# A hand-written order of work in the attention slots of a transformer layer: row maxima joined at part 53, projections in parts 44 to 47, reciprocals at 45 and 46 and at part 0 of the next slot

## The reference, cut to what matters

```python
q = split_heads(x @ Wq.T + bq)
k = split_heads(x @ Wk.T + bk)
v = split_heads(x @ Wv.T + bv)
q_lr = jnp.einsum('bhtd,hdr->bhtr', q, Wq_lsr)
k_lr = jnp.einsum('bhtd,hdr->bhtr', k, Wk_lsr)
scores = jnp.einsum('bhir,bhjr->bhij', q_lr, k_lr) * scale
scores = jnp.where(causal_mask, jnp.float32(-jnp.inf), scores)
attn = jax.nn.softmax(scores, axis=-1)
y = jnp.einsum('bhij,bhjd->bhid', attn, v)
```

## Time and profile before

| | |
|---|---|
| median of 3 runs | 4275.05 us (4274.4 to 4277.15) |
| the profiled execution's own time | 4274.05 us |
| its span, first to last instruction | 4272.3 us |
| mean granted TensorE clock | 0.924 of full speed |
| busy: PE, DVE, ACT, POOL | 3743.8, 2262.9, 1473.4, 687.8 us |

### The profile page before, as it was taken

One profiled execution on the slowest core, in us unless ns is written; L12 is line 12 of the kernel. 1 busy time (PEld: TensorE's weight loads), 2 busy tenths in 40 slices (PEclk: granted clock), 3 DMA queues, 4 the chain that ended last, 5 costly groups with the idle time before them and its releaser, 6 DMA issues. The chain is left out here.

```text
span 4272.3 us, 57451 instructions
## 1 busy us (share of the span) xinstructions
PE 3743.8 (88%) x21481; PEld 2587.1 (61%) x21481; DVE 2262.9 (53%) x3990; ACT 1473.4 (34%) x2753; POOL 687.8 (16%) x859
## 2 busy tenths in 40 slices
PE   5898998998998989989989832799999999999990
PEld 3555555555555555555555422788888888888880
DVE  2565564664664655655646457444454444544445
ACT  1343442443443433434424400333333333333324
POOL 2021121121121211211211210011111111111100
PEclk8999999999999999999999965699999999999995
DMA  4224233133322332242331110333344333443328
GB/s 154 68 81 113 58 102 98 46 97 98 93 70 78 100 102 64 79 117 59 102 97 41 43 57 5 104 117 106 121 127 136 114 108 121 126 136 113 111 69 324
DMA packets 187321, 422.56 MB, mean 99 GB/s; under 512 B 39777, under 2 KB 42849, under 8 KB 178401
## 3 DMA queue, kind: packets, MB, share of 16 engines
q1 hardware_dynamic: 167408, 367.98, 28.7%
q0 software_dynamic: 14336, 34.09, 4.2%
q10 hardware_dynamic: 5376, 17.83, 1.0%
HBM read 245.70 MB, written 72.38 MB: 74 GB/s over the span
## 5 line engine op out<-in xcount | busy, mean ns | idle before, releaser
L841 DVE TENSOR_REDUCE max_slots<-shared_banks 128x1 f32<-128x512 f32 (+3 forms) x1536 | 786.0, 548 | 497.0 <-PE shared_banks L636 370.7
L792 ACT ACTIVATE probs<-scores_t 128x512 f32<-128x512 f32 (+3 forms) x1536 | 671.4, 492 | 661.5 <-PE scores_t L678 653.1
L1510 PE MATMUL m_ps_h<-m_tokens_t,m_w_parts 128*128 128x512 f32 x3072 | 740.0, 391 | 1.6 <-DVE m_tokens_t L1448 1.6
L1510 PE MATMUL m_ps_y<-m_w_parts,m_hidden_parts 128*128 128x512 f32 x3072 | 737.0, 390 | 0.5
L678 PE MATMUL scores_t<-q_operands,k_operands 128*128 128x512 f32 (+3 forms) x1536 | 570.5, 412 | 114.3 <-DMA q_operands<-minus_max 108.3
L1510 PEld LDWEIGHTS m_ps_y<-m_w_parts,m_hidden_parts 128*128 128x128 f32 x3072 | 575.5, 188 | 125.3 <-issue 6.3
L1510 PEld LDWEIGHTS m_ps_h<-m_tokens_t,m_w_parts 128*128 128x128 f32 x3072 | 575.6, 188 | 120.1 <-issue 2.0
L633 PE MATMUL shared_banks<-k_operands,q_operands 96*128 96x512 f32 (+3 forms) x1536 | 555.0, 392 | 13.8 <-DVE natural L834 7.9
L1417 ACT ACTIVATE m_hidden<-m_ps_h,m_b 128x512 f32<-128x512 f32 x256 | 176.6, 690 | 817.8 <-PE m_ps_h L1510 804.6
L678 PEld LDWEIGHTS scores_t<-q_operands,k_operands 128*128 128x128 f32 x1536 | 294.0, 207 | 237.0 <-DMA q_operands<-minus_max 114.9
L633 PEld LDWEIGHTS shared_banks<-k_operands,q_operands 96*128 96x128 f32 x1536 | 314.5, 206 | 193.2 <-issue 138.2
(11 more groups left out here) (202 smaller groups left out, 3139.4 us busy)
## 6 DMA issues: line engine op xcount, KB each, us to landing
m_w_raw<-in_w1T SPq DMA_DIRECT2D x64, 1024.0 KB, 5.1
m_w_raw<-in_w2T SPq DMA_DIRECT2D x64, 1024.0 KB, 7.9
q_operands<-natural SPq DMA_DIRECT2D x384, 128.0 KB, 2.7
k_operands<-natural SPq DMA_DIRECT2D x384, 128.0 KB, 2.7
wqk_group<-scratch_wqk SPq DMA_DIRECT2D x32, 1024.0 KB, 5.2
natural<-in_xT SPq DMA_DIRECT2D x8, 2048.0 KB, 9.1
x_residual<-in_x SPq DMA_DIRECT2D x64, 256.0 KB, 2.7
scratch_x<-probs SPq DMA_DIRECT2D x64, 256.0 KB, 2.0
```

Of the source, the lines that this page charges most:

```text
L792: act.activation(probs[:, slot_of(k, h // 2), h % 2, c0:HALF], st[:, (HG * k + h) % SCORE_BANKS, c0:HALF], ACT.Exp, scale=SCALE).then_inc( ...
L841: dve.tensor_reduce(mx[:, h, slot:slot + 1], src[:, 0:n], AX.X, ALU.max).then_inc(bank_free[bank], 1)
L1510: mm = pe.matmul(bank, a, b, start=(first and n == 0), stop=(final and n == len(pairs) - 1))
```

## The change

Three tables of the order are replaced; no instruction is added or removed. The join moves from behind part 58 to behind part 53, the four projections from 47, 49, 50, 50 to 44, 47, 47, 47, the reciprocals of a slot's first half from 40, 44, 48, 49 to 45, 45, 45, 46, and the fourth reciprocal of the second half from part 14 of the next slot to part 0. The 48 maxima are spread anew: two now follow part 0, and the last comes behind part 50 instead of part 55.

```diff
-MAX_AFTER = (0, 2, 2, 0, 1, 2, 0, 1, 2, 0, 2, 0, 1, 0, 1, 2, 0, 0, 0, 1,
-             0, 3, 1, 0, 1, 1, 1, 0, 1, 0, 2, 1, 1, 0, 1, 1, 1, 1, 1, 1,
-             0, 3, 0, 1, 0, 1, 1, 1, 1, 1, 0, 1, 1, 0, 1, 1, 0, 0, 0, 0)
-PROJ_AFTER = (47, 49, 50, 50)
-JOIN_AFTER = 58
-INVERT_AFTER = ((40, 44, 48, 49), (0, 0, 0, 14))
+MAX_AFTER = (2, 2, 1, 1, 1, 0, 1, 0, 1, 2, 1, 1, 0, 1, 0, 2, 1, 0, 0, 1,
+             1, 2, 0, 0, 3, 0, 0, 1, 2, 2, 0, 1, 1, 1, 0, 0, 3, 1, 2, 1,
+             0, 2, 1, 2, 1, 0, 0, 1, 0, 1, 1, 0, 0, 0, 0, 0, 0, 0, 0, 0)
+PROJ_AFTER = (44, 47, 47, 47)
+JOIN_AFTER = 53
+INVERT_AFTER = ((45, 45, 45, 46), (0, 0, 0, 0))
```

## The result

Over four runs the changed kernel takes 4331.36 us (4326.37 to 4332.35), beside 4275.18 for the kernel before on the same chip: a ratio of 1.0128, with an interval of 1.0111 to 1.0146. That is 56 us slower, where 35 were forecast. The profiled execution took 4331.96 us with a span of 4330.2 at a mean clock of 0.921, against 4274.05, 4272.3 and 0.924, so the traces have 57.9 us to account for.

The account below looks back on a forecast made before the run. TensorE was taken as the bound, with 103 us idle at boundaries waiting for row-maximum DMAs. 22.3 - 1.2 + 13.9 = +35.0 on 4274.05 gave 4309, with the median's 1.0 then 4310 us; range 4286 to 4338.

Parts of the forecast that it names:

- ACT's hold: On ACT at the join, exponentials queue behind two DMA issues: 2.14 us held, 2.44 from transpose to last score.
- the last score's shift: In each slot, 0.61 us of maxima moved ahead of the join plus 1.38 lost there: last score 1.99 us later.
- The strips bind: At boundaries, the first maximum waits for SP's six strips, starting 5.9 us after the last score; 0.69 us gained.
- The boundary's sum: Per boundary inside sequences, 1.99 - 0.69 - 0.33 = +0.97 us; over 23 boundaries +22.3.
- x: Time from the join's transpose to the slot's last score, forecast 2.44 us; whole sum 31x - 40.6, zero at 1.31.
- the clock's cost: TensorE's half clock behind boundary stalls, taken as unchanged; bounded by 0.9 x 23, or 20 us either way.
- third rival: The clock falls longer: each of 23 boundaries gets another 3.5 us at half clock, +40, or 4350 us; chance 0.10.
- The last boundary: In the last sequence, without strips: a 2.87 us stall goes, 1.77 of hold comes; with 0.1 for a wait, -1.2.
- the tails: Seven fourth slots joining for the next sequence, residual rows behind strips on SP: each moves by 1.99 us, +13.9 in all.
- the bound for a lost cover: Four reciprocals at part 0, hidden by the strips' stall; without that cover bounded by 0.4 us a boundary, 9 us.
- The input's split: Before the third slot's first projection: slack about used up, cost taken as 0, bounded by 1 us in 7 slots.
- The other side: ACT is held less between join and part 54's exponential: 31 us per microsecond of x, 4247 to 4275 us; chance 0.08.

Follow-up runs that it names:

- x3: The changed kernel with SP instead of ACT issuing the two row-maximum DMAs, ahead of its strips: 4309.67 us, ratio 1.0084.
- x4: The changed kernel with SP sending each head's six strips after that head's last score instead of all after part 57: 4294.91 us, ratio 1.005.
- fill runs: Four kernels with throwaway matmuls added in stalls: changed kernel 4302.89 us, kernel before 4245.48, x5 4219.73, x6 4249.87.
- x1: The changed kernel with the join put back behind part 58, its other edits kept: 4280.60 us, ratio 1.0011.
- x6: x4 with the second half's four reciprocals behind parts 4, 5, 6 and 14 instead of part 0: 4249.57 us, ratio 0.9942.
- x5: The kernel before with SP sending each head's six strips after that head's last score: 4253.56 us, ratio 0.995.
- x10: x6 with 6 throwaway matmuls before part 57's score and 4 before a slot's first maximum: 4249.87 us, ratio 0.9941.

## Why the prediction was right, and where it was short

The direction, the mechanism and the places of the two large stalls were as forecast, and 4331 lies inside the range. (The range, 4286 to 4338, is narrower than its own terms added up, 4282 to 4354.) 35 us were forecast and 57.9 came in the traces.

- **ACT's hold: right.** ACT takes its next instruction 2.20 us after the transpose (2.14 forecast), and the last score comes 2.53 after it (2.44). x3 shows that the hold is made of the issues and their wait. The rival by which the issue overlaps with the exponentials is refuted by 810.65 in the timeline: no exponential starts before both DMAs are issued. The Trainium skill, "DMA: Bandwidth & Descriptors", section "Issuing engines are not separate DMA queues", calls the sequencer's time to initiate a DMA usually small beside the DMA. That doesn't fit here: the two issues make 1.17 of the 2.80 us to the landing and 1.17 of ACT's 2.20, and counting them as nothing would have given no change.
- **The maxima moved and the last score's shift: right.** 1.99 us were forecast, and the first slots, which have no boundary in them, got longer by 14.6 / 8 = 1.82.
- **The strips bind: right, a little low.** Sixth strip issued to the first maximum's start: 2.53, and from the first strip 5.64; forecast was 5.9 from the last score, and it is 6.06. x4 confirms the chain: with strips by head the first maximum starts 3.69 after the last score.
- **The boundary's sum: the failed term.** +0.97 was forecast, and 1.85 measured: 20 us of the miss of 23. Idle time is up by 1.39 a period (4.48 to 5.87), 0.42 more than forecast, from the 0.09 in x, the 0.16 in the strips and 0.19 of small waits: 10 us. The rest, 0.47 or 11 us, is busy TensorE that took longer. The step that failed is "I take the clock's cost as it is today". The busy time at half clock went from 5.14 to 6.42 us a period, and half of the 1.28 is 0.64, enough to account for it. It is inside the 20 us that the prediction allowed, in the direction of its third rival, and far under that rival's 3.5 us of low clock. The fill runs agree by periods (9 us), and their whole times can't tell so little. So the clock's share is about 10 us by the traces, and it is not shown in whole times.
- **The last boundary and the tails.** Counted as a period, the last boundary was forecast at -1.2 less the 1.99 by which the last score ahead of it comes later, -3.2, and -0.3 came: 3 us of the miss. Nearly all of it is the new stall of 2.62 in the last slot. The prediction had costed it at nothing, as the masks behind the normalising are "needed only at part 8"; without a wait for strips in front, part 8 comes too soon for that. The tails moved as a whole and kept their length, as forecast.
- **Costed at nothing.** At the 23 boundaries the reciprocals at part 0 were hidden, as the timeline shows and as x1's 5 us allow, but not in the last slot; and the bound for a lost cover was wrong by a factor of five (x4 against x6). The ring's three banks do not hide a late reduction: TensorE stood 1.46 us for it in x4. The input's split cost 2.6 us in three waits, within its 7.
- **The other side.** No run came out faster with the join at 53 until the strips were let go by head and the reciprocals were spread (x6).

## What to carry to other kernels

Before a step with DMA issues in it is moved earlier on an in-order engine, list what then queues behind it, and look for a second chain that ends just behind the stall to be removed: both together may cost more than the stall. Release a group of transfers by the finest event that frees each of them; one wait divided by head gave 21 us here to the kernel before and 36 to the changed one. Work that a stall hides has a price as soon as the stall is mended, so cost it again with each mend, and for every place where the stall is missing, such as a last slot.

## What the runs showed of the hardware that I had not expected

Filling a known stall with throwaway matmuls paid: 27 us on the kernel before and 34 more on x5, with the low clock almost gone from the periods. It paid nothing on x6 (x10), where TensorE ran into other waits instead, so time at half clock is not worth half of itself everywhere.

Issuing is dear in both queues that were tried: two 16 KB transfers take ACT 1.17 us and SP 1.16. Moved from the one to the other (x3) they put SP's strips back by 1.19 us a slot, and of the 50 us expected 22 were gained.
